# The first five expert weight copies issued ahead of the wait for the scatters, and row loads moved next to their own weight copy

## What is computed

```python
ys = _geglu(xf @ Ws1 + bs1) @ Ws2 + bs2                 # shared expert
logits = (xf @ Wr + br) / TAU
top_val, top_idx = jax.lax.top_k(logits, 2)             # 2 of E = 12 experts
top_w = jax.nn.softmax(top_val, axis=-1)
w = jnp.einsum('nke,nk->ne', jax.nn.one_hot(top_idx, E), top_w)
h = jnp.einsum('nd,edh->enh', xf, We1) + be1[:, None, :]   # D = 128, 2*HR = 768
yE = jnp.einsum('enh,ehd->end', _geglu(h), We2) + be2[:, None, :]
yr = jnp.einsum('end,ne->nd', yE, w)
return (ys + yr).reshape(B, T, Dm)
```

## Time and profile before

| | before |
|---|---|
| median of three runs | 470.45 us |
| lowest and highest | 469.33 and 470.94 us |
| profiled execution | 469.14 us, span 467.4 us |
| PE matmul busy | 405.8 us (87% of the span) |
| DVE, ACT, POOL busy | 313.4, 273.0, 271.0 us |
| weight copies (L1100) | 75 of 384 KB |
| row loads (L1093) | 75 of 68 KB |

### The profile page before, as it was taken

One profiled execution on the slowest core, in us unless ns is written; L12 is line 12 of the kernel. 1 busy time (PEld: TensorE's weight loads), 2 busy tenths in 40 slices (PEclk: granted clock), 3 DMA queues, 4 the chain that ended last, 5 costly groups with the idle time before them and its releaser, 6 DMA issues.

```text
span 467.4 us, 9975 instructions
## 1 busy us (share of the span) xinstructions
PE 405.8 (87%) x2658; PEld 321.1 (69%) x2658; DVE 313.4 (67%) x1057; ACT 273.0 (58%) x648; POOL 271.0 (58%) x360
## 2 busy tenths in 40 slices
PE   0176799998989897999998698999999999999991
PEld 0133466765655583877666698999999999999530
DVE  4669889999999999644831555555655555655162
ACT  2476599998978766595532354455545555554055
POOL 4766757586567867788777543444444444444264
PEclk9997789999999898999999599999999999999997
DMA  5389900000001000111132566666666666764393
GB/s 153 90 169 356 280 1 0 1 1 2 0 2 42 24 31 14 44 37 48 61 108 67 181 225 222 233 232 241 243 233 239 228 230 231 249 234 174 120 325 113
DMA packets 49261, 64.09 MB, mean 137 GB/s; under 512 B 9916, under 2 KB 32188, under 8 KB 49208
## 3 DMA queue, kind: packets, MB, share of 16 engines
q1 hardware_dynamic: 44760, 54.08, 34.8%
q0 software_dynamic: 4448, 9.38, 6.0%
HBM read 20.87 MB, written 13.91 MB: 74 GB/s over the span
## 4 chain that ended last, share of the span: by engine, by line
PE 54%; DVE 12%; POOL 12%; issue 9%; DMA 5%; ACT 4%; SPq 2%; ACTq 0%; DVEq 0%; POOLq 0%
PE bank L1244 23%; PE bank L1262 11%; POOL dispatched_rows L407 7%; PE bank L956 4%; PE bank L974 4%; PE bank L907 2%; PE bank L908 2%; DVE bst L478 2%; PE bank L1236 2%; PE bank L985 1%; DMA xnT_all<-routed_rows 1%; PE bank L986 1%; POOL rstd L817 1%; POOL frs L817 1%; ACT z L683 1%
## 5 line engine op out<-in xcount | busy, mean ns | idle before, releaser
L1133 POOL DMA_INDIRECT routed_rows<-yo,goes_to x75 | 71.8, 958 | 102.3 <-DVE yo L1172 99.6
L1244 PE MATMUL bank<-xT,w 128*128 128x128 f32 x900 | 119.6, 284 | 5.8 <-DMA w<-we_sb 3.9
L1244 PEld LDWEIGHTS bank<-xT,w 128*128 128x128 f32 x900 | 108.9, 195 | 8.3 <-issue 5.8
L1208 ACT ACTIVATE gl<-bank,tile_bias 128x128 f32<-128x128 f32 x225 | 66.7, 365 | 60.3 <-PE bank L1244 59.3
L1165 DVE SCALAR_TENSOR_TENSOR actT<-bank,tile_bias,gl 128x128 f32<-128x128 f32 x225 | 65.7, 345 | 31.4 <-PE bank L1244 25.4
L407 POOL DMA_INDIRECT dispatched_rows<-rows_all,slot_i x64 | 64.2, 1003 | 18.5 <-issue 17.3
L1262 PE MATMUL bank<-we_sb,actT 128*128 x450 | 62.7, 276 | 1.0 <-DVE yo L1172 0.9
L1262 PEld LDWEIGHTS bank<-we_sb,actT 128*128 128x128 f32 x450 | 56.1, 192 | 1.4 <-issue 1.4
L1172 DVE TENSOR_SCALAR yo<-bank,goes 128x128 f32<-128x128 f32 x75 | 26.3, 350 | 33.6 <-PE bank L1231 33.4
L956 PE MATMUL bank<-xk,wfk_sb 128*128 128x512 f32 x64 | 34.2, 649 | 5.2 <-DVE xk L575 4.2
L1202 ACT ACTIVATE xT<-bank 128x128 f32<-128x128 f32 x75 | 20.8, 277 | 28.9 <-PE bank L1236 28.2
(11 more groups left out here) (204 smaller groups left out, 824.2 us busy)
## 6 DMA issues: line engine op xcount, KB each, us to landing
w<-we_sb SPq DMA_DIRECT2D x75, 384.0 KB, 2.7
x_all<-dispatched_rows SPq DMA_DIRECT2D x75, 68.0 KB, 2.0
we_sb<-we SPq DMA_DIRECT2D x1, 4608.0 KB
rows_all<-x SPq DMA_DIRECT2D x8, 256.0 KB, 2.7
x_all<-routed_rows SPq DMA_DIRECT2D x8, 256.0 KB, 4.8
xnT_all<-routed_rows SPq DMA_DIRECT2D x8, 256.0 KB, 6.6
out<-x_all SPq DMA_DIRECT2D x8, 256.0 KB, 2.3
routed_rows<-yo,goes_to POOLq DMA_INDIRECT x75
```

What stands on the lines that cost most here:

```text
L1133: ng.indirect_dma_start(routed, bass.IndirectOffsetOnAxis(ap=goes_to[n // U % DB][:, n % U:n % U + 1], axis=0), yo[n % YO][:, :], None).th ...
L1208: na.activation(gl[n % 2][:, j * P:(j + 1) * P], ps_g[j][:, 0:P], ACT.Gelu, bias=tile_bias[:, HK + j, n:n + 1]).then_inc(s2["gelu_ready"], 1)
L1244: return nt.matmul(to[:, 0:P], w1[m][:, off:off + P], xT[m][:, :], start=True, stop=True)
```

## The change

On SP, the weight copies of tiles 0 to 4 are issued as soon as `tiles_known` is raised, ahead of the waits for `dispatched` and `pads_placed`. The row loads of tiles 0 to 4 follow these waits. The loop for the remaining tiles then goes from 5 to 74, and in it the row load of tile n stands just ahead of the weight copy of tile n. In the kernel before, the loop went from 0 to 74, with the weight copy of tile n ahead of the row load of tile n+5. `load_rows` and `load_weights` themselves, and the program of every other engine, are unchanged.

```diff
             for n in range(E):
                 to = sp.value_load(pad_at[0:1, n:n + 1], min_val=0, max_val=E * REGION - P)
                 sp.dma_start(dispatch[ds(to, P), :], pad_rows[n * P:(n + 1) * P, :]).then_inc(s2["pads_placed"], 16)
-            sp.wait_ge(s2["tiles_known"], 1)
-            sp.wait_ge(s["dispatched"], SLOTS // P * 16)
-            sp.wait_ge(s2["pads_placed"], E * 16)
-
             def load_rows(n):
...
+            sp.wait_ge(s2["tiles_known"], 1)
+            for n in range(U):
+                load_weights(n)
+            sp.wait_ge(s["dispatched"], SLOTS // P * 16)
+            sp.wait_ge(s2["pads_placed"], E * 16)
             for n in range(U):
                 load_rows(n)
-            for n in range(TILES):
+            for n in range(U, TILES):
+                load_rows(n)
                 load_weights(n)
-                if n + U < TILES:
-                    load_rows(n + U)
```

## The result

The changed kernel took 544.3 us (542.73 to 545.15, 4 runs) against 470.11 us of the kernel before on the same chip (4 runs). The ratio is 1.157, with a 95% interval of 1.154 to 1.161. Forecast were 537 us and a range of 508 to 551.

A forecast was written before the change was run, and what follows sets the result against it. PE was taken to set the pace of the tile loop, SP nearly as slow. From the median 470.45 us: less 0.6 (start), plus 50.3 (order), plus 17.0 (clock) gives 537.15, say 537 us; range 508 to 551.

The forecast's parts named there:

- The start: Seam before the tile loop: five weight copies ahead of the waits gain 0.6 us, between +1.6 and -1.4.
- the late row of before: One row load in the kernel before, issued at 280.95, landed after 3.55 us and delayed two turns by 2.13 us.
- The landing of the last scatter: At the seam, copies beside the last scatters delay the last one by 1.0 us, bounds 0 and 3.
- The order: Tile loop: row loads come too late for DVE in 14 rounds, 3.74 us each; 50.3 us lost in all.
- the landing of the row load: Step in each loop stall: the row load's landing taken at median 2.0 us, bounds 1.8 and 3.6.
- the prediction's own sign: Tile loop: the prediction is wrong if, among other signs, the stall has another length than 3.2 us.
- The clock: PE's clock halves for 3.4 us after stalls in 10 of 14 rounds: 17.0 us lost, between 0 and 23.8.
- The clock that holds in every round: Rival, tile loop: same stalls but no fall of PE's clock, 520.2 us; chance 0.16.
- The clock that falls in every round: Rival, tile loop: PE's clock falls after all 14 stalls, 544 us; chance 0.14.
- Slack on DVE: Rival, tile loop: DVE has activations ready ahead and absorbs the later rows, 468.9 us; chance 0.06.
- The copies were early: Seam: copies out at about 253.1, before the last scatter lands; the rival that they are not, 537.8 us, chance 0.04.
- the forecast DVE waits: Tile loop: DVE's L1150 waits for row loads some 14 times, about 4.1 us each, together near 57 us.

The follow-up runs named there:

- The idle matmuls: The changed kernel plus four unread PE matmuls between gate and up matmuls of each round's last tile: ratio 1.118; on another chip 527.84 us, ratio 1.120.

## Why the prediction was right

**The start** was put at 0.6 us gained, between +1.6 and -1.4. The early copies alone measured 2.6 us faster, and 0.6 with the 2.1 of the late row of before added would be 2.7. But the traces do not divide the gain that way. The turn that closes the up matmuls of tile 3 came at 271.42 in the kernel before, at 272.74 in the changed kernel and at 272.06 in the early copies alone, and their last scatters began at 251.56, 252.18 and 251.63. With this taken off, the changed kernel is 0.7 us later at that turn and the early copies alone are 0.6 later. By one trace of each kernel, the start thus lost some 0.6 to 0.7 us where 0.6 gained was forecast.

The landing of the last scatter was sized well (1.04 us longer; the 1.0 taken was an estimate), and the activations of tile 0, not the weight copy, became the wait, as forecast. The term that was missing is the clock at the seam. PE now starts earlier and stops 1.68 us for these activations, which it did not do before, and the tile behind the stop ran near half clock and took 3.85 us. Before, it ran at full clock and took 2.22. The two windows, before and after:

```profile
266.97:269.19 2.22, 2.22 (x22) 1.00 0.63 221
```

```profile
266.56:270.41 3.85, 3.85 (x23) 0.58 0.40 138
```

The gain of the early copies comes in the loop. From that turn to the last one the kernel before took 157.51 us and the early copies alone 154.27, and the late row is not among its delays. With the five copies out of the way SP runs further ahead. The row load of tile 14, the late one of before, went out at 280.95, 1.66 us ahead of the turn at 282.61. In the early copies alone:

```profile
276.09 0.34 SPq L1089 DMA_DIRECT2D x_all<-dispatched_rows  x1
```

```profile
283.22 0.27 PE L1238 MATMUL bank<-ident,x_all 128*128 128x128 f32 x1
```

That is 7.13 us ahead. That the sum of 0.6 and 2.1 meets the 2.6 is in part luck.

**The order** was put at 50.3 us. The mechanism is shown from three sides. The order alone costs 73.0 us; DVE asking later removes some 70 us of the loss with SP's order left as it is; and two tiles more of lead bring the loss to nothing. The size of the term can be read where the clock did not interfere: in the two rounds without a fall the pairs of turns took 8.11 and 8.06 us, with landings of 1.86 and 1.82. That is 3.65 and 3.60 us lost per round, against the forecast 3.74 at a landing of 2.0. The term was low in the landing of the row load. It was taken as 2.0 us from the earlier trace rows and had a mean of 2.39 in the 14 decisive loads, which is 14 x 0.39 = 5.5 us more. PE's waits for the activations in the 14 stalls came to 51.9 - 1.7 = 50.2 us, 3.6 us each against the 3.2 forecast, and that landing is the larger part of the difference. So by the prediction's own sign the stall has another length than it said. The other steps of the path came out as written in the first stall: 0.21 us from the end of the last up matmul, at 272.91, to the copy (0.05 and 0.2), 1.10 from copy to load (1.08), and 1.25 from landing to PE (1.25). Over the 14 rounds the load went out 1.64 us after the turn on average, against 1.50 in the sum.

**The clock** was put at 17.0 us for 10 of 14 rounds, 1.7 each. It fell in 12, and in two of these it stayed low about twice as long. What one fall cost can be read within the last seven rounds. Three with stalls of 2.82 to 2.98 us and a single fall took 9.46 to 9.68 us for the pair, and the two without a fall, after stalls of 2.95 and 2.90, took 8.11 and 8.06. That is 1.5 us for a fall. The idle matmuls gave back 14 to 18 us, with falls left in 2 rounds. What remains of the loss once the start as forecast and the order with its longer landing are taken off is 73.85 + 0.6 - 55.8 = 18.7 us (the 73.85 is 544.3 less the 470.45 of the forecast), about 1.6 us per fall. This remainder also holds the errors of the other terms.

**The rivals.** The clock that holds in every round (520.2) is refuted by the windows of the changed kernel; it does hold, in 13 of 14 rounds, with one tile more of lead, where the gaps are 1.8 us or less. The clock that falls in every round (544, with 6.8 us for the four rounds at 1.7 that the sum left out) came nearest in time, but not for its reason: two rounds did not fall, and the landing made up the rest. Slack on DVE was found nowhere in the changed kernel. The copies were early, as forecast, with the first at 247.56 and the last out by 252.94, ahead of the last scatter's landing at 255.49. The first expert matmul came at 259.74, just past the 259.5 that was written. Ahead of the stalls the forecast DVE waits were 57 us and the page has 68.6 for the 14 (77.9 less the 9.3 at the start), because both the landing and the low clock behind a stall move DVE's own start.

Of the miss of 7.2 us (544.3 less 537.15) 5.5 are landing. The other 1.7 is a remainder, in which the start (lost, not gained), the later issue of the loads, the clock and the small delays that the kernel before had in its own loop stand together; the runs do not divide it further. The landing, the start and the clock lie within the bounds that stood in the text.

## What to carry to other kernels

When a transfer is moved on an in-order queue, ask of each transfer behind it which wait it now stands behind, and who asks for it first: here a row load fell behind a wait for PE, and its first reader was not PE's transpose, two tiles ahead, but a small operation of DVE that takes a whole round of rows at once. Count the lead of each load in steps of its earliest reader; the first tile more of lead was worth some 48 us here (70 to 22 on one chip), and the next one some 23. The early weight copies that the change was named for are a gain of 0.4 to 0.6% once they stand in the old order of the loop. By the traces they give it by letting SP run further ahead in the loop, while at the seam itself they win nothing until POOL's additions are out of DVE's way.

## What was not expected of the hardware

A stop of PE cost more than its length: with 3.6 us of waiting the two turns around a stall came 5.56 us late on average. Four idle matmuls in each stop made the kernel faster by 3 to 4% of the time before. Gaps of up to 1.8 us, once in each round, left the loop's granted clock at 0.97, with a fall behind one of them (the turn after it took 3.51 us, 2.61 to 2.74 after the others), and gaps of 2.8 to 4.6 us brought it to 0.89.

Small DVE operations on a few columns took 1.19 us beside POOL's additions and 0.17 without them, the cast of 128x5 too, which has only one input. The activations (one operand in PSUM, 128x128) kept their 0.87 us for three beside the same additions, in the kernel whose additions were moved back:

```profile
263.93 0.87 DVE L1168 SCALAR_TENSOR_TENSOR actT<-bank,tile_bias,gl 128x128 f32<-128x128 f32 x3 [1.33 <-PE bank L1247]
...
270.59 1.18 DVE L1160 CAST goes_to<-goes 128x5 uint32<-128x5 f32 x1
```
